# Four small moves in a four-stage transformer kernel: the third stage's context transposes issued later, five load buffers for its weights, a wait for a ones column put at its use, and the router's loads put first

## The reference, cut to what matters

```python
x = x + tanh(g_xattn[0]) * L0_xattn(layernorm(x), ctx, masks, ...)   # stage one: softmax attention
x = x + tanh(g_ffn[0])   * L0_ffn(layernorm(x), w_fc, w_proj)        # stage two
x = x + tanh(g_xattn[1]) * L1_xattn(layernorm(x), ctx, ...)          # stage three
x = x + tanh(g_ffn[1])   * L1_ffn(layernorm(x), ...)                 # stage four: shared + routed experts

def L0_ffn(x, w_fc, w_proj):                 # bitlinear: layer norm, absmax clip, ternary weights
    h = gelu(bitlinear(x, w_fc))             # 512 -> 2048
    return bitlinear(h, w_proj)              # 2048 -> 512

def L1_xattn(query, kv, Wq, Wg, bg, Wkv, Wo):            # linear attention
    q = query @ Wq.T; gate = sigmoid(query @ Wg.T + bg)
    k, v = split(kv @ Wkv.T)
    q, k = phi(q), phi(k)                                # phi(x) = x + 1 if x > 0 else exp(x)
    kv_summary = einsum('bhsd,bhse->bhde', k, v); k_sum = k.sum(-2)
    attn = (q @ kv_summary) / (q . k_sum + EPS)
    return (attn * gate) @ Wo.T
```

## Time and profile before

| what | us |
|---|---|
| runs shown: lowest, median, highest (3 runs) | 1680.8, 1681.04, 1686.86 |
| profiled execution: time | 1678.48 |
| profiled execution: span, first to last instruction | 1676.7 |
| TensorE busy in the span | 1579.1 |
| mean granted TensorE clock, share of full speed | 0.984 |

### The profile page before, as it was taken

One profiled execution on the slowest core, in us unless ns is written; L12 is line 12 of the kernel. 1 busy time (PEld: TensorE's weight loads), 2 busy tenths in 40 slices (PEclk: granted clock), 3 DMA queues, 4 the chain that ended last, 5 costly groups with the idle time before them and its releaser, 6 DMA issues. The chain is left out here.

```text
span 1676.7 us, 29168 instructions
## 1 busy us (share of the span) xinstructions
PE 1579.1 (94%) x10826; PEld 827.4 (49%) x10826; DVE 974.4 (58%) x1947; ACT 710.3 (42%) x1311; POOL 824.1 (49%) x853
## 2 busy tenths in 40 slices
PE   5889999999889999899999989999999999999998
PEld 3456666565544444345556544444444444444443
DVE  5756676778748999835655543377564333322246
ACT  3288887888885556523232221211111111133321
POOL 3488887877864445433543434344342442022234
PEclk9899999999799999999999999999999999999999
DMA  7764544323344554434454426455553755287856
GB/s 187 170 124 100 112 99 114 90 62 74 92 96 94 120 123 104 91 79 89 98 120 91 79 71 162 101 122 132 98 123 79 151 123 107 77 191 190 191 146 193
DMA packets 453955, 195.66 MB, mean 117 GB/s; under 512 B 395501, under 2 KB 418287, under 8 KB 453817
## 3 DMA queue, kind: packets, MB, share of 16 engines
q1 hardware_dynamic: 448136, 175.19, 46.8%
q0 software_dynamic: 5680, 18.62, 4.4%
HBM read 77.17 MB, written 22.81 MB: 60 GB/s over the span
## 5 line engine op out<-in xcount | busy, mean ns | idle before, releaser
L1143 POOL TENSOR_TENSOR a_pl<-a_prob,a_ph 128x512 f16<-128x512 f32 x256 | 295.4, 1167 | 73.9 <-ACT a_prob L1032 73.3
L1232 DVE TENSOR_REDUCE a_mx<-bank 128x2 f32<-128x512 f32 x256 | 173.1, 686 | 86.8 <-PE bank L730 85.1
L140 PE MATMUL bank<-XTh,d_whs 128*128 128x512 f16 x512 | 194.7, 380 | 3.8 <-PEq L89 2.4
L141 PE MATMUL bank<-XTl,d_whs 128*128 128x512 f16 x512 | 194.8, 380 | 0.0
L142 PE MATMUL bank<-XTh,d_wls 128*128 128x512 f16 x512 | 194.8, 380 | 0.0
L1031 ACT ACTIVATE a_ph<-bank 128x512 f16<-128x512 f32 x256 | 153.8, 601 | 59.7 <-PE bank L750 33.0
L2434 POOL CAST d_cut<-d_raw 128x512 f16<-128x512 f32 x90 | 55.8, 620 | 227.8 <-DMA d_raw<-in_L_ffn_sw 146.0
L1032 ACT ACTIVATE a_prob<-bank 128x512 f32<-128x512 f32 x256 | 154.2, 603 | 0.0
L2354 DVE TENSOR_TENSOR d_hid<-d_hid,bank 128x512 f32<-128x512 f32 x64 | 43.9, 686 | 168.0 <-PE bank L142 164.1
L2345 ACT ACTIVATE d_hid<-bank 128x512 f32<-128x512 f32 x64 | 38.2, 597 | 204.7 <-PE bank L142 204.7
L2349 ACT ACTIVATE d_hh<-d_hid 128x512 f16<-128x512 f32 x64 | 40.3, 629 | 193.3 <-DVE d_hid L2354 193.3
(11 more groups left out here) (348 smaller groups left out, 3994.3 us busy)
## 6 DMA issues: line engine op xcount, KB each, us to landing
d_raw<-in_L_ffn_w SPq DMA_DIRECT2D x48, 256.0 KB, 3.0
d_raw<-in_L_ffn_sw SPq DMA_DIRECT2D x42, 256.0 KB, 3.1
made<-e_y SPq DMA_DIRECT2D x39, 256.0 KB
a_stage<-in_L_ffn_w_fc SPq DMA_DIRECT2D x32, 256.0 KB, 2.9
a_stage<-in_L_ffn_w_proj SPq DMA_DIRECT2D x32, 256.0 KB, 3.1
a_fbuf<-in_ctx SPq DMA_DIRECT2D x16, 256.0 KB, 3.2
rows<-f_cut SPq DMA_DIRECT2D x16, 256.0 KB, 2.4
out_x<-X SPq DMA_DIRECT2D x16, 256.0 KB, 2.4
```

Source lines behind the costliest of these rows:

```text
L140: nc.tensor.matmul(out_ap, lhi, rhi, start=first, stop=False)
L141: nc.tensor.matmul(out_ap, lhi, rlo, start=False, stop=False)
L1143: nc.gpsimd.tensor_tensor(pl[:, n % NP, :], prob[:, n % 2, :], ph[:, n % NP, :], ALU.subtract).then_inc(ev["L"], 1)
L1232: nc.vector.tensor_reduce(mx[:, h, tt, half, 2 * (g % 4):2 * (g % 4) + 2], bank[BS + m % 2][:, :].rearrange("p (r k) -> p r k", r=2), AX_X ...
```

## The change

Stage two's ring `craw` has five buffers instead of three. The four context transposes of batch 0 are no longer issued in SP's turn 10; the first two (high and low of the first 128 rows) are issued in turn 12 and the other two in turn 13, each behind the hidden tile of its turn. In stage three TensorE waits for c_one ahead of the first batch's sums and no longer ahead of everything. In stage four SP issues the two router loads ahead of the three piece loads. In stage one the three chains on VectorE become one with one semaphore.

```diff
@@ stage one @@
-        tlink = Chain(dve, t_ch)
+        tlink = nlink
...
-        flink = Chain(dve, f_ch)
+        flink = nlink
@@ stage two @@
-    NG, RG = 5 * KC, 3
+    NG, RG = 5 * KC, 5
...
-            if n == CNEXT - 3:
-                for t in range(2):
-                    cols, rows = slice(t * P, (t + 1) * P), slice(t * P, (t + 1) * P)
-                    sp.dma_start_transpose(CTh[:, :, 0, cols], ctx_hi[rows, :]).then_inc(c_ct[0], 16)
-                    sp.dma_start_transpose(CTl[:, :, 0, cols], ctx_lo[rows, :]).then_inc(c_ct[0], 16)
+            if n in (CNEXT - 1, CNEXT):
+                rows = slice((n - CNEXT + 1) * P, (n - CNEXT + 2) * P)
+                sp.dma_start_transpose(CTh[:, :, 0, rows], ctx_hi[rows, :]).then_inc(c_ct[0], 16)
+                sp.dma_start_transpose(CTl[:, :, 0, rows], ctx_lo[rows, :]).then_inc(c_ct[0], 16)
@@ stage three @@
-            pe.wait_ge(c_one, 1)
-
...
                 for n in ("pK0", "pK1", "cV0", "cV1"):
                     wait(n, b)
+                if b == 0:
+                    pe.wait_ge(c_one, 1)
@@ stage four @@
+            sp.dma_start(rw[:, :], a["L1_ffn_router_w"]).then_inc(r_in, 16)
+            sp.dma_start(ebias[:, :], env["row"](a["L1_ffn_expert_bias"])).then_inc(r_in, 16)
             for i in range(RING):
                 sp.dma_start(as_loaded(raw[:, i, :], i), of_piece(i)).then_inc(p_in[i], 16)
-            sp.dma_start(rw[:, :], a["L1_ffn_router_w"]).then_inc(r_in, 16)
-            sp.dma_start(ebias[:, :], env["row"](a["L1_ffn_expert_bias"])).then_inc(r_in, 16)
```

More of the change, by code:

```diff
@@ L379, in phase_a @@
     fq = sb("a_fq", [P, 2, 3])
-    f_ch, f_var, f_rs, f_nm, f_xn, f_cl, f_hi, f_lo = (sem("af_" + n) for n in (
-        "chain", "var", "rstd", "nmean", "normed", "clipped", "hi", "lo"))
+    f_var, f_rs, f_nm, f_xn, f_cl, f_hi, f_lo = (sem("af_" + n) for n in (
+        "var", "rstd", "nmean", "normed", "clipped", "hi", "lo"))
     f_tp = [sem(f"af_turned{i}") for i in range(2)]
@@ L429, in phase_a @@
     s_in = [sem(f"t_in{i}") for i in range(NST)]
-    t_use, t_mag, t_part, t_tot, t_red, t_ch = (sem("t_" + n) for n in (
-        "use", "mag", "part", "tot", "red", "chain"))
+    t_use, t_mag, t_part, t_tot, t_red = (sem("t_" + n) for n in (
+        "use", "mag", "part", "tot", "red"))
     t_tp = [sem(f"t_turned{i}") for i in range(2)]
```

## The result

The changed kernel takes **1689.06 us** in the median of eight runs (1679.19 to 1691.72), the kernel before 1681.01 (1677.26 to 1686.86, eight runs beside them). The ratio is **1.0041, 95% interval 1.0022 to 1.0059**: slower by 6.9 us (3.7 to 9.9); the two medians as they stand are 8.1 apart, and the text goes by the ratio. The forecast was +4.3 us and 1685.3; the range holds the result. By its estimate it lies within 0.5%, though the interval reaches just beyond.

What follows compares the result with a forecast made beforehand. The prediction took VectorE's 15.71 us a tile to bound stage two, though TensorE was busy 94% of the span. Its parts summed 0 + 5.6 + 0 - 1.3 + 0 = +4.3 us, giving 1685.3 us, range 1677.9 to 1690.5.

Steps and rivals of the forecast that it cites:

- Part 1: Stage two, five buffers for the weights' loads: cost 0, as VectorE's 15.71 us a tile hides the gain.
- rival B: Stage two: five buffers pay, 5.5 us of waits and 1.9 of clock come off; total -3.1 us, chance 0.05.
- Part 2: Stage two's tail, context transposes moved later: new 9 us wait at the first context product, +3.7 and 1.9 clock, +5.6 us.
- the upper bound: Context transposes' move in stage two: +8.9 us, if two transposes take 2.59 us and a landing is 0.7 slower.
- Rival C: SP's queue in stage two's tail: four context issues take 2.6 us instead of 1.3; total +9.5 us, chance 0.09.
- Part 3: Stage three's start, later wait for the ones column: what the queries win is lost at the sums, cost 0.
- Part 4: Stage four's start, router's loads first: the bias lands 1.3 us sooner, gain 1.3 us, bounds 0 and 1.6.
- TensorE is the bound from there on: Stage four after down projection 0: claimed TensorE sets the pace, behind the 1.3 us gain taken from the router's loads.
- Part 5: Stage one, one chain semaphore for three: all run on VectorE in program order and await the same instruction, cost 0.
- the wait of 7 to 10 us: Stage two: sign that the forecast is right, TensorE waiting at the first context product, with lower clock behind it.
- Rival A: Stage two's tail: context lands before 724.0, down 14 starts 4.3 us sooner; total -5.6 us, chance 0.12.

Runs made afterwards that it cites:

- e5: Kernel before with only five buffers for the weights' loads and the merged chain on one semaphore: -0.3 us (-3.2 to +2.4).
- e7: Kernel before with one extra bn_stats on VectorE right ahead of its clip in turns 2 to 11 of stage two: -1.5 us (-4.2 to +1.2).
- e6: Kernel before with only the router's two loads put ahead of the three weight loads in stage four: +1.2 us (-1.3 to +3.7).
- e4: Changed kernel with the four context transposes issued one a turn in turns 4 to 7: -1.2 us (-3.5 to +1.3) against the kernel before.
- e8: Kernel before with only the four context transposes issued one a turn in turns 4 to 7: -3.4 us (-6.2 to -0.5).
- e11: Kernel before with VectorE's next front moments ahead of its hidden clip, five load buffers and the merged chain: -10.1 us (-13.0 to -7.2).
- e3: Changed kernel with all four context transposes behind hidden tile 13 (turn 12): +2.2 us (-0.3 to +4.7) against the kernel before.

## Why the prediction was right

**Part 1, cost 0: right, and borne out.** The load waits vanish, waits for the hidden tile take their place, and e5 is at -0.3 us. The reason was too short in one point: I called VectorE the bound, and e7 shows that VectorE has 0.7 us a tile to spare; what bounds is its round with ScalarE. The page "Perfetto Trace Analysis" of the Trainium skill, section "Optimization Strategy", names too few buffers as what the same gap repeated can mean, and rival B took it at its word. Here it was not the cause, by e5's -0.3 us: the gap came from another engine.

**Part 2, +5.6: right in mechanism, low in size.** Every step of the rebuilt queue came in its order. Against it, offset taken off: down 12 at 702.5 (forecast 702.0), down 13 at 718.1 (717.1), the first context product at 734.1 (733.0), down 15 at 753.5 (752.2). One term was mis-sized, and it stood in the upper bound only: the transpose at 715.46 took 2.45 us instead of 1.27, on the queue's path, 1.2 us. The clock cost 2.15 instead of 1.9. 5.6 plus these is 7.0; stage two shows 6.9. Rival C's mechanism, issues that take longer, was thus there once, for a quarter of its price. It was no chance either: each of the fourteen profiled kernels has such an issue among the eight transposes of hidden 13. In the kernel before it does no harm, as TensorE wants that tile only at 722.42 (timeline of SP's queue before):

```profile
716.57 2.42 SPq L1483 DMA_TRANSPOSE b_hTl<-b_hcut  x1
```

The changed queue has no such slack, so this 1.2 us belonged in the forecast and not only in its bound.

**Part 3, cost 0: right.** Timeline of TensorE after, at the third stage's start:

```profile
768.49 0.27 PE L140 MATMUL bank<-c_xh,c_wh 128*128 128x256 f16 x1 [3.00 <-PEq L89]
...
775.19 2.02 PE L1982 MATMUL bank<-c_v,c_k 128*128 128x129 f32 x16 [1.30 <-issue]
```

The wait of 3.0 us at the queries had never been for the ones column: taken away, another releaser is named for the same wait. The sums come 6.70 us later, 6.73 before. Not run alone.

**Part 4, -1.3: wrong, it is 0.** The step that failed is "TensorE is the bound from there on". In e6 down 0 did come 1.5 us sooner, but behind a wait of 2.08 us, as long as the one removed, and the lower clock behind it cost 1.7 us, where before it had cost 1.5 ahead of down 0. I priced the wait and not the clock, which part 2 had taught me to price. In the changed kernel the turn does not wait at all (I forecast 0.7), and what it has won by the gate it has lost again at the choice of the tokens. Over runs e6 is at +1.2 (-1.3 to +3.7), so it is the traces that put the part at nothing.

**Part 5, cost 0: not told from zero.** It is inside e5's -0.3. Stage one took 516.5 us in the mean of the seven profiled kernels with the merged chain (514.4 to 518.9) and 514.4 in that of the seven without (511.4 to 517.6). These ranges overlap; it was not run alone, so a cost of a microsecond or two stays open.

The sum: 1.3 that part 4 did not give and 1.4 of part 2's size bring the forecast of +4.3 to +7.0; measured +6.9, with an interval (3.7 to 9.9) that would hold 4.3 and 5.6 as well, so the agreement to a tenth is luck. The two misses point the same way and did not cancel. The sign, the place and the wait of 7 to 10 us were as written. Rival A was false here, since the context landed 9 us after TensorE came for it, and its 4.3 us at down 14 came once the context was early (4.7 in e4), though only 2.7 of it were kept. The advice of the page "DMA: Bandwidth & Descriptors" of the Trainium skill, section "Rules for kernel authors", to issue early and wait late spoke against the part, and e8's -3.4 us agrees with it; by it alone I would have missed why the old place was bad too.

## What to carry to other kernels

A transfer that is moved must be followed through its queue to its reader: here two issues behind the next tile's eight made a 9 us wait, four in a row cost whichever tile stood behind them, and one a turn, early, cost nothing. When an engine has the same small wait in every round, ask which round it closes, and put work that is ready into the wait: a swap of two calls gave more than all buffers. A removed wait is worth what its successor leaves, and a stall that drops TensorE's clock cost 1.5 to 2.2 us more than its length here. An issue that takes longer at one place of a queue can stand at the same place in the next kernel: look for it in the trace before, also where it does no harm there.

## What the runs showed of the hardware that was not expected

- Of SP's 155 to 163 transposes in stage two (515 to 765 us) five to nine take 1.6 to 2.7 us instead of 1.27: 6 of 157 before, 6 of 157 after, 8 of 159 in e4, there from 568.98 on every 26 to 31 us. They are not scattered: counted from the stage's start, all fourteen profiled kernels have one at 3.1 us, one at 54 to 57 us and one in hidden tile 13 (187 to 206 us). On the queue's path they cost their 0.8 to 1.2 us in full. What makes them is open.
- The lower clock came behind waits of 1.8 us (e11, the router's turn) to 8.88 us (after), and where I worked it out it cost 1.5 (before, ahead of down 0), 1.7 (e6, down 0), 1.7 (e3, down 14), 1.9 (before, down 12) and 2.15 us (after, the context). It did not come behind every such wait: down 11 ran at full clock behind 2.93 us in e3, 2.99 in e4 and 3.03 in e5. In the fourth stage it came right behind the opening wait of 2.44 us in seven of the fourteen profiled kernels, and only behind a second wait of 1.8 to 2.1 us in the other seven, with the same opening wait. The first gate product is at 11.3 to 11.9 us in the former and at 12.7 to 13.1 in the latter. What decides is open.
- Stages that hardly an edit touches differ between executions by more than the effect looked for (stage one 511.4 to 518.9, 511.4 to 517.6 with the very same code), so a few us can be read in the stage where they act, and hardly in one profile's span.
